# Reordering the out-projection, the first chunk and the softmax copies of a Mamba, cross-attention and feed-forward layer

## The reference

```python
# x (2, 2048, 512), ctx (2, 77, 512), mask (1, 1, 2048, 77); layer norms have no weights
# 1. selective scan: INNER = 1024 channels, 16 states
xz = x @ W_in + b_in;  x_proj, z = split(xz)
u = silu(x_proj);  B, C = split(u @ W_xproj + b_xproj);  dt = softplus(u @ W_dt + b_dt)
h_t = h_{t-1} * exp(dt_t * A) + dt_t * u_t * B_t;  y_t = sum_states(h_t * C_t) + D * u_t
o = (y * silu(z)) @ W_out + b_out
x1 = layernorm(x + o)
# 2. cross-attention, 16 heads of 32, 77 keys per batch
q, k, v = x1 @ Wq.T + bq, ctx @ Wk.T + bk, ctx @ Wv.T + bv
x2 = layernorm(x1 + softmax(mask(q k.T / sqrt(32))) v @ Wo.T + bo)
# 3. feed-forward, 2048 hidden
hid = x2 @ W1 + b1
hid = hid + phase * w_imag * sin(theta + 0.1 * hid) * 0.1
out = layernorm(x2 + relu(hid) @ W2 + b2)
```

## Time and profile before

| | us |
|---|---|
| median of 3 runs | 3333.94 (3333.69 to 3336.71) |
| the profiled execution, its own time | 3333.15 |
| its span, first to last instruction | 3331.4 |
| PE busy | 2877.4 (86%) |
| DVE busy | 2689.6 (81%) |
| ACT busy | 2013.8 (60%) |
| POOL busy | 1833.0 (55%) |
| mean granted TensorE clock | 0.945 of full speed |

### The profile page before, as it was taken

How to read it: one execution, slowest core, us unless ns; L and a number is a source line. 1 busy time by engine, 2 the same in 40 slices (tenths; PEclk the granted TensorE clock), 3 DMA queues, 4 the chain that set the end, 5 groups by cost and what they waited for, 6 DMA issues and landing times. The chain is left out here.

```text
span 3331.4 us, 48893 instructions
## 1 busy us (share of the span) xinstructions
PE 2877.4 (86%) x18996; PEld 1288.0 (39%) x18996; DVE 2689.6 (81%) x3063; ACT 2013.8 (60%) x3622; POOL 1833.0 (55%) x950
## 2 busy tenths in 40 slices
PE   5888878889889889889788887888889998999998
PEld 2222222222222222222222225555556666666665
DVE  3899999999999999999999885555556776667765
ACT  4676776776677677767667543444445555555554
POOL 3697988988978979878879982211111111111100
PEclk8999999999899899999999897999999999999999
DMA  4111112111111111111121435111100000010000
GB/s 148 51 45 49 56 39 66 48 51 42 48 61 48 36 58 48 54 42 54 48 83 42 149 100 195 50 40 40 40 30 24 21 21 21 21 35 27 22 7 14
DMA packets 120118, 172.77 MB, mean 52 GB/s; under 512 B 13265, under 2 KB 48721, under 8 KB 119378
## 3 DMA queue, kind: packets, MB, share of 16 engines
q1 hardware_dynamic: 119890, 169.63, 15.8%
HBM read 100.92 MB, written 66.58 MB: 50 GB/s over the span
## 5 line engine op out<-in xcount | busy, mean ns | idle before, releaser
L780 POOL TENSOR_TENSOR h<-h,c_rep 128x1024 f32<-128x1024 f32 x512 | 1198.8, 2355 | 271.3 <-ACT carry L566 270.6
L713 DVE TENSOR_TENSOR_SCAN h<-r_ps,carry,h 128x512 f32<-128x512 f32 x768 | 942.5, 1272 | 8.3 <-ACT r_ps L560 8.0
L560 ACT ACTIVATE r_ps<-r_ps,decay 128x512 f32<-128x512 f32 x1024 | 631.2, 656 | 353.9 <-PE r_ps L338 353.5
L700 DVE TENSOR_TENSOR h<-u_ps,b_rep 128x1024 f32<-128x1024 f32 x512 | 618.8, 1209 | 59.8 <-PE u_ps L349 58.2
L349 PE MATMUL u_ps<-dtu,spread 32*128 32x512 f16 x2048 | 319.6, 391 | 104.7 <-DVE h L700 104.1
L1769 POOL TENSOR_TENSOR o_in<-o_in,rows 128x1024 f32<-128x1024 f32 x15 | 36.4, 2426 | 620.0 <-DMA o_in<-o_dram 620.0
L338 PE MATMUL r_ps<-dt,spread 32*128 32x512 f16 x2048 | 313.9, 386 | 57.6 <-DVE h L713 44.8
L361 PE MATMUL y_ps<-h,gather 128*32 128x512 f32 x2048 | 288.2, 631 | 61.2 <-POOL h L780 61.2
L713 DVE TENSOR_TENSOR_SCAN h<-r_ps,zero,h 128x512 f32<-128x512 f32 x256 | 314.1, 1271 | 7.8 <-ACT r_ps L560 7.7
L40 PE MATMUL fps<-x,region 128*128 128x256 f16 x1024 | 279.9, 273 | 3.5 <-issue 2.4
L42 PE MATMUL fps<-x,region 128*128 128x256 f16 x1024 | 279.3, 273 | 0.0
(11 more groups left out here) (246 smaller groups left out, 5772.7 us busy)
## 6 DMA issues: line engine op xcount, KB each, us to landing
u_t_dram<-u SPq DMA_DIRECT2D x16, 1024.0 KB, 4.9
z_t_dram<-zs SPq DMA_DIRECT2D x32, 512.0 KB, 3.0
uz<-u_t_dram SPq DMA_DIRECT2D x64, 256.0 KB, 3.8
uz<-z_t_dram SPq DMA_DIRECT2D x64, 256.0 KB, 4.2
y_t_dram<-y SPq DMA_DIRECT2D x64, 256.0 KB, 2.4
region<-y_t_dram SPq DMA_DIRECT2D x32, 256.0 KB, 3.5
result<-x SPq DMA_DIRECT2D x16, 512.0 KB, 2.8
x_t<-dram_x_t SPq DMA_DIRECT2D x15, 512.0 KB, 3.9
```

The source lines that it names most:

```text
L560: nc.scalar.activation(bank, bank, ACT.Exp, scale=decay[:, col:col + 1]).then_inc(s_da, 1)
L700: nc.vector.tensor_tensor(h[:, g % H_GROUPS, o:o + 2, :], u_ps[:, :, :], b_rep[:, c % 2:c % 2 + 1, :].broadcast_to([P, 2, TS]), ALU.mult). ...
L713: nc.vector.tensor_tensor_scan(row, r_ps[:, 2 * (pair % 2) + o, :], row, start, ALU.mult, ALU.add)\
L780: nc.gpsimd.tensor_tensor(rows, rows, c_rep[:, c % 2:c % 2 + 1, :].broadcast_to([P, 2, TS]), ALU.mult)\
```

## The change

1. In the scan phase the last pair's weighing by C goes from POOL to DVE, and POOL's two additions to the first rows go from s = 60 and 61 to s = 38 and 42.
2. In `first()` the keys of both batches come from one pass (154 columns per matmul instead of twice 77), and the orders of PE, ACT, DVE and SP are written anew: the probabilities and their copies come before evictions and parameters, and y's tile 1 and the weight pieces are loaded in another order. `OPS_FIRST` falls from 3 to 2: `first()` has tiles 0 to 3.
3. `OPS_UNTIL` goes from 6 to 7: the bodies 1 to 6 have pairs m = c + 1. In the bodies from 2 on, PE does the two tiles behind `hidden(b, 5)` and `hidden(b, 6)`, into `sps`; in body 1 behind `hidden(b, 1)`. The evictions of these pairs go to two buffers that lie in `p_t` (`out_ring`), and ACT waits for both stores (`ring_stored`) before it copies probabilities there.
4. In all bodies with an attention part ACT copies the transposed probabilities earlier, right behind `relu(b, 4)` and `sine(b, 5)`. DVE makes the exponentials' sums apart from the normalisation (`exp_sums`), and does `fraction(b, 5)` before the second tile's normalisation.

```diff
-OPS_FIRST, OPS_UNTIL = 3, 6
+OPS_FIRST, OPS_UNTIL = 2, 7
+Y_PAIRED = 6
# PE, scan phase: sums(g) of the last group waits for s_hl too; DVE, behind the last scans:
+            dve.wait_ge(s_carry, TOTAL)
+            rows = h[:, (TOTAL - 1) // 2 % H_GROUPS, 2:4, :]
+            nc.vector.tensor_tensor(rows, rows, c_rep[:, (NC - 1) % 2:(NC - 1) % 2 + 1, :].broadcast_to([P, 2, TS]), ALU.mult)\
+                .then_inc(s_hl, 1)
# POOL, scan phase
-                weigh(pair)
+                if pair < TOTAL - 1:
+                    weigh(pair)
...
-                if s == 60:
+                if s == X0_AT:
...
-                if s == 61:
+                if s == X0_AT + 4:
# (X0_AT = 38)
+        def keys_psum(t):
+            return nat[:, t // 2, t % 2 * BATCH * CTX:(t % 2 + 1) * BATCH * CTX]
+        out_ring = [p_t[:, 4 * n:4 * n + 4, :].rearrange("p h t -> p (h t)") for n in range(NT)]
# SP
+            def next_y(i):
+                sp.wait_ge(s_yl, i)
+                load_y(i + (1 if i >= Y_PAIRED else 2) - 1)
...
             def first():
+                load_y(0)
+                load(b_q[:, :], a["b_q"], s_small)
                 load_mask(0, 0)
+                load_piece(2)
...
+                load_next(0, 0)
                 for s in range(2):
                     load(w_out[:, s, :, :], a["w_in_rows"][:, :, 2 * D + s * D:2 * D + s * D + D], s_wout)
-                load_next(0, 0)
-                for n in range(2, 6):
+                load_y(1)
+                for n in range(3, 6):
                     load_piece(n)
...
+                next_y(1)
+                next_y(2)
+                load_piece(6)
+                store_projection(0, o_out[:, :])
+                next_y(3)
+                load_piece(7)
...
             def body(c, par, batch, front, late, ops, more):
+                if not late:
+                    next_y(Y_PAIRED - 1)
+                    store_projection(OPS_FIRST * NT - 1, o_out[:, :])
+                elif ops:
+                    next_y(ops[0] * NT + 1)
                 if more:
                     sp.wait_ge(s_rwo, c * NT)
                     load(x1[:, 1 - par, :, :], chunk_rows("x", c + 1), s_xin)
...
                 for m in ops:
+                    if late and m < CHUNKS - EARLY_OUT - 1:
+                        next_y(m * NT + 2)
                     for t in range(NT):
...
+                        store_projection(m * NT + t, out_ring[t])
# PE, first()
+                keys()
                 x1_transposed(0, 0)
-                values(0)
+                values(0, (0, 1), False)
                 queries(0)
...
-                out_projection(0, 1, nat)
-                probs_t(0, 0, (0, 1, 2, 3))
+                probs_t(0, 0, (0, 1))
+                out_projection(0, 1, nat, 0, 3)
+                probs_t(0, 0, (2, 3))
+                out_projection(0, 1, nat, 3, 6)
...
# PE, body()
                 hidden(b, 0)
-                for m in ops:
-                    out_projection(c, m * NT, sps)
-                    out_projection(c, m * NT + 1, sps)
...
                 hidden(b, 5)
+                if late:
+                    for m in ops:
+                        out_projection(c, m * NT, sps)
                 second(b, 2)
                 hidden(b, 6)
+                if late:
+                    for m in ops:
+                        out_projection(c, m * NT + 1, sps)
                 second(b, 3)
                 if front:
+                    if late:
+                        for m in ops:
+                            pe.wait_ge(s_oe, m * NT + 2)
                     probs_t(c, 0, (0, 1))
# ACT
+            def ring_stored(m):
+                act.wait_ge(s_ost, (m + 1) * NT * 16)
# ACT, body(), behind hid_out(b, 5) and relu(b, 4)
+                if late:
+                    for m in ops:
+                        out_evacuated(m * NT, sps)
+                if front and not ops:
+                    probs_out(c, 0, (0, 1))
                 sine(b, 5)
+                if front and not ops:
+                    probs_out(c, 0, (2, 3))
                 hid_out(b, 6)
-                if front:
+                relu(b, 5)
+                for m in ops:
+                    if late:
+                        out_evacuated(m * NT + 1, sps)
+                    ring_stored(m)
                     probs_out(c, 0, (0, 1))
-                relu(b, 5)
-                sine(b, 6)
+                if ops:
+                    sine(b, 6)
+                    probs_out(c, 0, (2, 3))
+                if front:
+                    values_high(c, 0)
+                    probs_out(c, 1, (0, 1))
+                if not ops:
+                    sine(b, 6)
+                if front:
+                    probs_out(c, 1, (2, 3))
                 hid_out(b, 7)
# DVE, body()
                 if front:
+                    exp_sums(c, 0)
                     probabilities(c, 0)
                 mix(b, 4)
                 if front:
-                    probabilities(c, 1)
+                    exp_sums(c, 1)
                 act_low(b, 4)
                 fraction(b, 5)
+                if front:
+                    probabilities(c, 1)
                 mix(b, 5)
```

More of the change, by code:

```diff
@@ L944, in attention_ffn_phase @@
                   in zip(a["early_pieces"], (w_q, w_o))]
-        for name, w, k_step in (("w_1", w_1, 1), ("w_2", w_2, 4)):
-            for k in range(0, w.shape[2], k_step):
+        for name, w, k_step, order in (("w_1", w_1, 1, (1, 3, 0, 2)), ("w_2", w_2, 4, (0, 4, 8, 12))):
+            for k in order:
                 stage = stages[(len(pieces) - 2) % 4].rearrange("p (k n) -> p k n", k=k_step)
@@ L1140, in keys, with values @@
                                   start=(k == 0), stop=(k == KD - 1))
                 last.then_inc(s_kvp, 1)
-            def values(batch):
+            def values(batch, ks, bias):
                 out = fps[0:CTX, batch, :, :].rearrange("p i t -> p (i t)")
-                for k in range(KD):
+                for k in ks:
                     mm(out, ctx_t[:, k, batch, :], wv[:, k, :], start=(k == 0), stop=False)
-                mm(out, ones, b_v, start=False, stop=True).then_inc(s_kvp, 1)
+                if bias:
+                    mm(out, ones, b_v, start=False, stop=True).then_inc(s_kvp, 1)
@@ L1444, in body @@
                 b, d = c - 1, c - 2
-                if not late:
-                    out_evacuated(2 * OPS_FIRST - 2, nat)
-                for m in ops:
-                    y_high(m * NT)
+                if late:
+                    for m in ops:
+                        y_high(m * NT)
                 deviation("wo", 1, c)
@@ L1463, in body @@
                     deviation("x1", 0, c + 2)
-                if not late:
-                    act.wait_ge(s_wlo, len(pieces))
-                for m in ops:
-                    y_high(m * NT + 1)
-                hid_out(b, 0)
-                for m in ops:
-                    out_evacuated(m * NT, sps)
-                    out_evacuated(m * NT + 1, sps)
-                hid_out(b, 1)
+                if late:
+                    for m in ops:
+                        y_high(m * NT + 1)
+                else:
+                    act.wait_ge(s_wlo, len(pieces))
+                hid_out(b, 0)
+                hid_out(b, 1)
+                if not late:
+                    for m in ops:
+                        out_evacuated(m * NT, sps)
+                        out_evacuated(m * NT + 1, sps)
                 sine(b, 0)
@@ L1684, in body @@
                 statistics("wo", 1, b, x2[:, 1 - par, :, :])
-                if not late:
-                    normalize("x1", 0, c, x1[:, par, :, :])
                 normalize("wo", 1, b, x2[:, 1 - par, :, :])
@@ L1795, in first @@
                 x1_sum(1, 1)
-                for i in range(1, OPS_FIRST * NT):
+                for i in range(1, Y_PAIRED - 1):
                     y_low(i)
             def body(c, par, batch, front, late, ops, more):
-                for m in ops:
-                    y_low(m * NT)
+                if late:
+                    for m in ops:
+                        y_low(m * NT)
                 if more:
```

260 lines of the change are left out of this document (137 added, 123 removed).

## The result

The changed kernel takes 3214.9 us (median of four runs, 3211.2 to 3220.7) against 3335.2 before (3333.7 to 3336.7): ratio 0.964, interval 0.962 to 0.966. The forecast was 3203, with a range of 3183 to 3243. The profiled execution took 3216.79 us, its span 3215.1, against 3331.4.

What follows compares the result with a forecast made beforehand. PE was taken as the bound, 93% busy in bodies without out-projection, its idle time led by the `p_t` wait. Savings 1.1 + 32 + 8.4 + 46.5 - 8.0 + 50.4 = 130.4 us gave 3203, range 3183 to 3243.

Steps and rivals of the forecast that it cites:

- the one stepped through: Bodies 7 to 15: probability copies ahead of `sine(5)` end PE's `p_t` wait; 5.6 us off each, ends 2.6 and 6.0.
- the low clock behind the gap: Bodies 7 to 15: slow clock after PE's `p_t` wait, 0.60 for 3.9 us, taken as some 1.5 us lost.
- Rival 1: 14 bodies: ScalarE replaces the stall, only 3 of 5.6 us come; +36 us, 3239; chance 0.12.
- Rival 3: 14 bodies: clock stays low in the stretch of transposes though the gap is gone; +21 us, 3224; chance 0.06.
- The new wait: Bodies 2 to 6, before PE's second scores: 3.2 us more stall on top of the existing 0.8.
- The tiles go behind `hidden(5)` and `hidden(6)`, where both low halves have long been made: Bodies 2 to 6: waits of 7.75 and 0.78 us and slow matmuls go; 10.4 us of tile work stays.
- The `p_t` gap goes: Body 1: the wait for copied probabilities vanishes, part of 8.4 us off (ends 3 and 14).
- `hidden(1)` (2.8 us) now fills part of it: Body 1: this work partly covers PE's 8.62 us wait for y_low; part of 8.4 us off.
- 1.1 us more for twice the columns: First chunk: merged key pass costs 1.1 us extra, saving 6.0 of the second pass's 7.11 (ends 0 and 7.1).
- Rival 2: First chunk held by loads of y and w_2: 14 us less there, 4 in body 1; 3221; chance 0.12.
- Rival 4: 14 bodies: copies still come late since another wait binds ScalarE; +78 us, 3281; chance 0.04.
- Rival 5: 14 bodies: PE, nearly gapless, gets the low clock; gain gone at 14% of work, 3360 at 17%; chance 0.02.

Runs made afterwards that it cites:

- both_orders: Kernel before, bodies 6 to 15 only: ScalarE copies probabilities ahead of sine(5), VectorE normalises the second tile behind fraction(5); 3270.0 us.
- before_y_early: Kernel before, one edit: in bodies 2 to 5 SP loads y's second tile at the body's start, not behind the result's store; 3300.0 us.
- combined: Changed kernel, tiles of bodies 2 to 6 before first scores, y's load behind x and o_in, body 1's chain and early copies, additions at s=60, 61; 3173.4 us.
- tiles_before_scores: Changed kernel, both tiles of bodies 2 to 6 ahead of the first scores, hidden(1) ahead of scores and early copies in all bodies; 3202.5 us.
- tiles_first: Changed kernel, tiles of bodies 2 to 6 ahead of first scores, hidden(1) behind them, early copies, bodies 7 to 15 as changed; 3184.3 us.
- keys_twice: Changed kernel with each 154-column key matmul split into two of 77; keys took 13.9 us, keys' start to first residual 9.7 us more.

## Why the prediction was right or wrong

**Bodies 7 to 15: right, and too small.** The mechanism is the one stepped through, shown by `both_orders`. The mis-sized term is the low clock behind the gap: I took 1.5 us from one window of 3.9 us; with a gap of 4.3, 6.6 us came, above my upper end of 6.0, so some 2.3 hung on the clock. Rival 1 (ScalarE binds) fell: no wait of PE on ScalarE is left there. Rival 3 fell too: the stretch with its transposes ran at 1.00. The Trainium skill's sentence that transposes do not count for the clock ("TensorE: Matmul & The Clock Gate", PE-mode transpose) can't be tested by this trace, in which transposes come in groups of 1 us among other matmuls. What I drew from it, a low clock in that stretch, did not come.

**Bodies 2 to 6: 79.7 forecast, 82.0 measured.** The new wait was foreseen at 4.0 us and was 4.7. What was not counted is the low clock behind it, 2.4 us in scores and `hidden(2)` (4.34 instead of 2.79), the same effect that I had counted behind every gap that I took away. Against these 3.1 us stands 1.0 from the body without tiles, which the sum starts from (66.1 forecast, 65.1 measured). The step "The tiles go behind `hidden(5)` and `hidden(6)`, where both low halves have long been made" named a place that was not needed: with the tiles where they were, an earlier load alone takes the wait for the low half away (`before_y_early`). By the rows the new place would have done it too, since in body 2 before the low half was ready at 2217.7 and the tiles' new place would come some 10 us later (estimate: `hidden(5)` ends at 2248.9, less the tiles, their waits and slow matmuls, about 21 us); no run has the new place with the old load. What the step left out is its price: the tiles' 10.4 us of work no longer cover the second scores' wait. The numbers close: 91.3 before, less 9.1 (`before_y_early`), less 6.4 (`both_orders`, measured on bodies without tiles) is 75.8, and `combined` has 76.0. Of what these two edits offer, the change as made gave 6.0 us a body back.

**Body 1: the largest miss of a single body, 9.8 us.** "The `p_t` gap goes" failed because I took body 1 for a body without tiles. It has `ops`, so ScalarE takes the branch that copies behind `relu(5)`, while PE's tiles stand elsewhere and cover nothing. The early copies alone are worth 6.4 us there (`tiles_before_scores`, `tiles_first`). "`hidden(1)` (2.8 us) now fills part of it" came about: the wait fell from 8.62 to 6.31 us. The rest of that wait hangs, by the rows, on terms left out: SP's store of tile 3 ahead of x and `o_in`, and VectorE and GpSimd side by side. And what the waits gave back the clock took: PE's idle time in the stretch fell by 2.5 us, but its busy time rose by 3.9 with the same 562 matmuls (73.7 to 77.6), at a clock of 0.91 instead of 0.94.

**First chunk: 32 off forecast, 38 measured.** I took 1.1 us more for twice the columns and so 6.0 off. At the same clock of 0.50 they cost 44 ns a matmul (257 against 213), 1.4 us for 32, so that term was nearly right. What the sum left out is the clock, which rises inside the one pass and lets what follows run faster: by `keys_twice` the one pass is worth 9.7 us and not 6.0. The Trainium skill's pace of columns over 1.2 GHz ("TensorE: Matmul & The Clock Gate", Back-to-back issue gap) would make the 77 more columns 64 ns, an estimate from that rule; the trace has 44. Rival 2, the loads, fell: y's second tile came at 2025.7, and PE did not wait for it. The other 2.5 us were not taken apart.

**End of the scan: -1.1 forecast, -1.2 measured** from gate to gate, stalls of 1.78 us instead of 1.85 included. The 5.7 us by which the attention part starts later than that lie in scan code that the change does not touch, in front of the additions; over the profiled kernels the gate that comes at 1874.2 before lies between 1874.1 and 1880.0. This, and 1.7 us of the last body in which the same 96 matmuls ran at 0.86 instead of 1.00, is what one execution differs from another by. What sets it stays open.

Summed by stretch against the forecast: +5.7 (scan), -6.0, +9.8, +11.6, -8.5, +1.7: 14 us above 3202.7 for the profiled execution. The misses on one side come to 28.8 us and on the other to 14.5; that they partly cancel, and the median lies only 12 us above 3203, is luck. Rival 4 fell for the bodies without tiles; in body 1 alone the copies did come late, but by the order that ScalarE was given and not by another wait. Rival 5 fell: the mean granted clock rose from 0.945 to 0.954.

## What to carry to other kernels

When a wait goes after an edit of several queues, move each queue's part alone: here an early load was enough to remove it, and the reordered matmuls uncovered the next one. Price every gap, removed or added, with the slower matmuls behind it: a gap of 4.3 to 4.7 us cost 2.3 to 2.4 more. Before the times of two passes are compared, compare their clocks. And read a flag such as `ops` for every body, the peeled ones first.

## What the runs showed of the hardware

VectorE and GpSimd slow each other: VectorE's weight splits took 3.97 us each (7.94 for two) instead of 2.28, GpSimd's sums 4.4 instead of 2.35, and a normalisation of 1.00 us took 2.81, ending with GpSimd's instruction. The Trainium skill ("SBUF — State Buffer", Who interferes with whom) says that a VectorE instruction with two SBUF inputs contends with GpSimd's reads, and that one which takes the shared ports blocks the other engine for its whole length; the trace agrees: beside VectorE's splits a sum of GpSimd's takes 4.4 us, nearly the two alone together (2.28 + 2.35).

The fp32 matmuls of the keys, each behind its own 128x128 weight load, started 213 ns apart with 77 columns and 257 ns apart with 154 at a clock of 0.50, and 131 ns apart with 154 at full clock (`keys_twice` and the changed kernel). What sets the 213 ns, the weight load or the instruction, is not shown.
